# 3rd and 4th attention: the mix with stationary values in four column tiles, both groups of heads in flight, and new turns

## The reference, cut to what matters

```
x -> norm -> 1st attention (8 heads x 32) -> + x -> norm, + a row per batch
  -> state scan over the 1024 rows (64 states, silu), + its output
  -> norm -> 2nd attention (16 heads x 64, causal) -> + x
  -> 3rd attention (16 heads x 16, masked twice) -> + x -> norm
  -> norm -> 4th attention (16 heads x 16, out-of-bounds mask) -> + x
  -> norm -> 256 -> 1024 -> gelu -> 256 -> + x

attention: q = h Wq + bq ; k, v = ctx Wk, ctx Wv
           p = softmax(q k^T / sqrt(hd)) over the 77 keys
           out = concat over heads(p v) Wo + bo
```

## Time and profile before

| | |
|---|---|
| median of 3 runs | 1373.24 us (1370.93 to 1376.13) |
| profiled execution, span from first to last instruction | 1373.0 us |
| PE busy | 1333.4 us, 97% |
| PE weight loads busy (beside PE) | 1124.9 us, 82% |
| DVE busy | 903.9 us, 66% |
| ACT busy | 674.3 us, 49% |
| POOL busy | 558.9 us, 41% |

### The profile page before, as it was taken

One profiled execution on the slowest core, in us unless ns is written; L12 is line 12 of the kernel. 1 busy time (PEld: TensorE's weight loads), 2 busy tenths in 40 slices (PEclk: granted clock), 3 DMA queues, 4 the chain that ended last, 5 costly groups with the idle time before them and its releaser, 6 DMA issues.

```text
span 1373.0 us, 23019 instructions
## 1 busy us (share of the span) xinstructions
PE 1333.4 (97%) x8771; PEld 1124.9 (82%) x8771; DVE 903.9 (66%) x2204; ACT 674.3 (49%) x1495; POOL 558.9 (41%) x700
## 2 busy tenths in 40 slices
PE   7999999999999999999999999999999999899999
PEld 5989987787888788878888888779877987688778
DVE  4778872776756766676576556784768467746771
ACT  4657766134554444544545435445344543464454
POOL 4465431107513643364346211572156216621661
PEclk9999999999999999999999999999999999999999
DMA  4334402200000000000000001000000000000000
GB/s 112 77 112 130 132 21 81 64 8 1 1 16 16 1 13 5 17 0 9 1 9 1 24 5 29 0 1 16 16 1 1 17 16 1 1 5 12 1 1 16
DMA packets 48463, 34.10 MB, mean 25 GB/s; under 512 B 22177, under 2 KB 45536, under 8 KB 48352
## 3 DMA queue, kind: packets, MB, share of 16 engines
q1 hardware_dynamic: 48304, 32.59, 8.5%
q10 hardware_dynamic: 48, 0.01, 0.0%
HBM read 23.26 MB, written 8.39 MB: 23 GB/s over the span
## 4 chain that ended last, share of the span: by engine, by line
PE 84%; DVE 6%; POOL 5%; SPq 2%; ACT 2%; issue 1%; DMA 1%; DVEq 0%; POOLq 0%; ACTq 0%
PE ps L886 11%; PE ps L876 10%; PE ps L836 10%; PE ps L932 8%; PE ps L943 8%; PE ps L855 8%; PE ps L846 6%; PE ps L896 5%; PE ps L802 5%; PE ps L785 4%; PE ps L1037 2%; SPq L611 1%; PE ps L1050 1%; POOL pr L1603 1%; POOL pr L1617 1%
## 5 line engine op out<-in xcount | busy, mean ns | idle before, releaser
L1578 POOL TENSOR_TENSOR rstd<-mv,halfneg 128x1 f32<-128x1 f32 x192 | 109.1, 570 | 340.7 <-DVE mv L1313 338.7
L1617 POOL TENSOR_TENSOR pr<-mx,pr 128x616 f32<-128x616 f32 x128 | 155.9, 1220 | 215.3 <-DVE mx L1347 213.9
L1158 ACT ACTIVATE pr<-pr 128x616 f32<-128x616 f32 x224 | 159.7, 715 | 145.9 <-POOL pr L1617 74.5
L1162 ACT ACTIVATE pr<-ps 128x512 f32<-128x512 f32 x224 | 132.7, 596 | 162.9 <-PE ps L855 162.7
L886 PEld LDWEIGHTS ps<-vtab,pr 128*128 128x128 f32 (+1 forms) x1280 | 153.0, 191 | 14.1 <-ACT pr L1162 10.5
L886 PE MATMUL ps<-vtab,pr 128*128 128x102 f32 (+1 forms) x1280 | 161.9, 275 | 2.0 <-ACT pr L1162 0.9
L855 PE MATMUL ps<-ident,pr 128*128 128x128 f32 (+1 forms) x1120 | 159.4, 275 | 3.5 <-POOL pr L1603 2.7
L1137 ACT ACTIVATE tt<-ps 128x256 f32<-128x256 f32 x160 | 60.9, 383 | 183.5 <-PE ps L785 183.4
L855 PEld LDWEIGHTS ps<-ident,pr 128*128 128x128 f32 (+1 forms) x1120 | 125.5, 139 | 30.1 <-POOL pr L1603 9.1
L876 PE MATMUL ps<-vwo,pr 128*128 128x256 f32 (+1 forms) x640 | 148.9, 381 | 0.0
L1411 DVE TENSOR_TENSOR xt<-xt,ps 128x256 f32<-128x256 f32 x192 | 79.7, 416 | 101.8 <-PE ps L896 50.4
(11 more groups left out here) (200 smaller groups left out, 2368.8 us busy)
## 6 DMA issues: line engine op xcount, KB each, us to landing
out_dram<-xt SPq DMA_DIRECT2D x64, 128.0 KB, 1.7
xt<-in_x_dram SPq DMA_DIRECT2D x32, 128.0 KB, 2.2
xt<-out_dram SPq DMA_DIRECT2D x32, 128.0 KB, 2.1
fc<-in_L_xattn_fc_w_dram SPq DMA_DIRECT2D x2, 1024.0 KB, 6.8
wk<-in_L_xattn_wkv_dram SPq DMA_DIRECT2D x4, 512.0 KB, 5.0
front<-in_L_xattn_wkv_dram SPq DMA_DIRECT2D x4, 512.0 KB, 5.9
wo<-in_L_xattn_wo_dram SPq DMA_DIRECT2D x1, 1024.0 KB, 5.2
kb<-in_L_xattn_wq_dram SPq DMA_DIRECT2D x1, 1024.0 KB, 6.8
```

What stands on the lines that cost most here:

```text
L1158: ac(v, v, ACT.Exp, scale=-ATTN[key[0]].scale).then_inc(done["expo"], 1)
L1162: ac(pr[:, run.lane, 0:4 * P], bank(run.lane, 0), ACT.Copy).then_inc(done["pturn_main"], 1)
L1617: p.tensor_tensor(p8, mx[:, run.lane, :].unsqueeze(2).to_broadcast([P, HG, KEYS]), p8, ALU.subtract).then_inc(done["below"], 1)
```

## The change

The mix of the 3rd and 4th attention swaps its operands. The values are stationary, 32 columns at a time (two heads of 16), and the transposed probabilities stream, 128 columns (the rows of the tile). Four products write the four quarters of the PSUM partitions, so that they lie in four column tiles of the array. A pair of heads spans 154 keys, which lie in two pieces, so each quarter is made by two products (`later` 0 and 1). The result has features on partitions: the turn of the heads and the path through `den_eps` and `heads` after the mix and the copies of the mix's columns go; ACT copies the result to `t` (`mixed`) for `proj`. The normalisation must come ahead of the mix: the 3rd attention gets `rowsum`, `den_eps`, `recip`, `weigh` on DVE, the 4th `rowsum` and `recip` on DVE and a new `scale` on POOL.

All three attentions of 16 heads now have both groups in flight: the second group has its own probabilities (`pr2`, in `front`), its own columns of `mx` and `rec`, its scores wait only for `shift` or `bound` of the first group, and one `mix` and one `resid` serve both. `front` being used for that, the value half of the 2nd attention's kv weights for the second pair is fetched only after the last key product of that pair. All four strings of `TURNS` and that of SP are new, phase 1 and the setup included.

```diff
-COPIES, WCOPY = (3, 2), 160
+SPLIT = 4
+WEIGHED = (L1, L2)
 def attention_steps(a):
...
+    first, second = f"{a.name}.0", f"{a.name}.1"
+    top = ["scores", "rowmax", "shift"] if a is L1 else ["scores", "bound", "rowmax", "below"]
+    masked = ["maskmul"] if a is L2 else []
+    norm = ["rowsum"] + ["den_eps"] * (a is L2) + ["recip", "weigh" if a in WEIGHED else "scale"]
+    turns = ["pturn", "pturn_main", "pturn_rest"]
     steps = [] if a is L1 else [("query", a.name), ("query_bias", a.name)]
...
+    steps += [(s, first) for s in top] + [("expo", first)] + [(s, second) for s in top]
+    steps += [(s, first) for s in masked + norm] + [("expo", second)] + [(s, first) for s in turns]
+    steps += [(s, second) for s in masked + norm + turns] + [("mix", a.name)]
+    return steps + ([] if a is L1 else [("mixed", a.name), ("proj", a.name)]) + [("resid", a.name)]
...
-            vtab[a.name] = sb("vtab" + a.name, [P, PAIR, a.groups, TSLOT[-1], a.hd + 1])
+            vtab[a.name] = sb("vtab" + a.name, [P, PAIR, a.groups, 2 * SPLIT, P // SPLIT])
...
-        vtmp = {"2": front[0:KEYS, 4096:4096 + PAIR * H].rearrange("p (b n) -> p b n", b=PAIR), "3": sb("vtmp3", [KEYS, PAIR, H])[:, :, :]}
+        vtmp = {"2": modrow[0:KEYS, 0:PAIR, :], "3": modrow[0:KEYS, PAIR:2 * PAIR, :]}
...
+        pr2 = front[:, 2048:2048 + LANES * 5 * P].rearrange("p (l n) -> p l n", l=LANES)
...
-                front[:, 0:4096].rearrange("p (k n) -> p k n", k=KC)]
+                front[:, 0:2048].rearrange("p (k n) -> p k n", k=KC)]
...
             def wkv1_get(key, run):
...
-                else:
+                elif part < WKV_PARTS // 2:
                     sp.wait_ge(done["vwo_mm"], at("vwo_mm", f"0{L1.groups - 1}{PAIR - 1}{TILES - 1}"))
...
+                else:
+                    sp.wait_ge(done["k_mm"], at("k_mm", f"11{L1.chunks - 1}"))
...
             def scores(key, run):
...
                 elif a is L1:
-                    pe.wait_ge(done["resid"], at("resid", "1.0", run))
-                else:
-                    pe.wait_ge(done["heads"], at("heads", f"{a.name}.0", run))
+                    pe.wait_ge(done["shift"], at("shift", "1.0", run))
+                else:
+                    pe.wait_ge(done["bound"], at("bound", f"{a.name}.0", run))
...
             def pturn(key, run):
...
+                if group(key):
+                    pe.wait_ge(done["pturn_main"], at("pturn_main", f"{a.name}.0", run))
+                    pe.wait_ge(done["pturn_rest"], at("pturn_rest", f"{a.name}.0", run))
+                elif a is not L0:
+                    s = "shift" if a is L1 else "bound"
+                    pe.wait_ge(done[s], at(s, f"{a.name}.1", run))
...
             def mix(key, run):
...
                     else:
-                        w = a.hd + 1
-                        dst = o[:, TFIRST[j] * w:(TLAST[j] + 1) * w]
-                        src = vtab[a.name][0:TROWS[j], b, g, TSLOT[j]:TSLOT[j + 1], :]
-                        if a is not L0:
-                            heads = TLAST[j] + 1 - TFIRST[j]
-                            n = COPIES[heads - 2]
-                            dst = o[:, 0:n * WCOPY].rearrange("p (k n) -> p k n", k=n)[:, :, TFIRST[j] * w:(TLAST[j] + 1) * w]
-                            src = src.rearrange("p s d -> p (s d)").unsqueeze(1).to_broadcast([TROWS[j], n, heads * w])
-                        last = mm(dst, pt, src, start=j == 0, stop=j == TILES - 1, skip_group_check=True)
+                        w = P // SPLIT
+                        for later in range(2):
+                            for two in range(SPLIT):
+                                j = two + later
+                                last = mm(o[two * w:(two + 1) * w, g * P:(g + 1) * P], vtab[a.name][0:TROWS[j], b, g, later * SPLIT + two, :],
+                                          pt[j], start=not later, stop=bool(later))
...
+            def mixed(key, run):
+                act.wait_ge(done["mix"], at("mix", key, run))
+                ac(t[:, run.lane, :, :].rearrange("p c n -> p (c n)"), bank(run.lane, 0)[:, 0:H], ACT.Copy).then_inc(done["mixed"], 1)
...
             def shift(key, run):
                 dve.wait_ge(done["rowmax"], at("rowmax", key, run))
...
+                if key == "1.1" and run.no == RUNS:
+                    dve.wait_ge(done["vwo_mm"], at("vwo_mm", f"0{L1.groups - 1}{PAIR - 1}{TILES - 1}"))
...
+            def scale(key, run):
+                pool.wait_ge(done["recip"], at("recip", key, run))
+                p8 = heads_view(key, run.lane)
+                p.tensor_tensor(p8, p8, each_head(rec, key, run.lane), ALU.mult).then_inc(done["scale"], 1)
```

More of the change, by code:

```diff
@@ L83, in attention_steps @@
 def attention_steps(a):
-    steps = [] if a is L1 else [("query", a.name), ("query_bias", a.name)]
[L85 to L96, removed]
-        else:
[L98 to L104, removed]
+    if a is L0:
+        steps = [("query", "0"), ("query_bias", "0")]
+        steps += [(s, "0.0") for s in ("scores", "rowmax", "shift", "expo", "pturn", "pturn_main", "pturn_rest", "mix", "recip", "heads")]
+        return steps + [("turn", "0o"), ("turned", "0o"), ("proj", "0"), ("resid", "0")]
+    first, second = f"{a.name}.0", f"{a.name}.1"
[3 more added lines that the diff above has]
+    turns = ["pturn", "pturn_main", "pturn_rest"]
+    steps = [] if a is L1 else [("query", a.name), ("query_bias", a.name)]
+    steps += [(s, first) for s in top] + [("expo", first)] + [(s, second) for s in top]
+    steps += [(s, first) for s in masked + norm] + [("expo", second)] + [(s, first) for s in turns]
+    steps += [(s, second) for s in masked + norm + turns] + [("mix", a.name)]
+    return steps + ([] if a is L1 else [("mixed", a.name), ("proj", a.name)]) + [("resid", a.name)]
 FIRST_NORM = [("load", "x")] + norm_steps("0") + [("prebias", "0")]
@@ L241 @@
[L241 to L245, removed]
@@ L539, in bank, with group, probs, heads_view @@
             return ps[:, 2 * lane + k, :]
+        def group(key):
+            return int(key[2])
+        def probs(key, lane):
+            return (pr2 if group(key) else pr)[:, lane, :]
+        def heads_view(key, lane):
+            return probs(key, lane)[:, 0:HG * KEYS].rearrange("p (h n) -> p h n", n=KEYS)
+        def each_head(small, key, lane):
+            return small[:, lane, group(key), :].unsqueeze(2).to_broadcast([P, HG, KEYS])
         def banks(lane):
@@ L681, in v0_put @@
                 sp.wait_ge(v0_zero, 1)
-                lay_values(sp, L0, vtmp0[:, two, :], vtab["0"][:, two, :, :, :], laid["0"])
+                lay_values(sp, L0, vtmp0[:, two, :], vtab["0"][:, two, :, :, :], laid[f"0{key}"])
             def v_lay(key, run):
@@ L1156, in expo @@
                 act.wait_ge(done[s], at(s, key, run))
-                v = pr[:, run.lane, 0:HG * KEYS]
+                v = probs(key, run.lane)[:, 0:HG * KEYS]
                 ac(v, v, ACT.Exp, scale=-ATTN[key[0]].scale).then_inc(done["expo"], 1)
@@ L1356, in rowsum @@
[L1356 to L1362 removed]
+                s = "maskmul" if key[0] == "2" else "expo"
+                dve.wait_ge(done[s], at(s, key, run))
```

258 lines of the change are left out of this document (134 added, 124 removed).

## The result

The kernel after takes 1398.78 us (median of 4 runs, 1395.1 to 1403.4) against 1372.14 for the one before: a ratio of 1.019, 95% interval 1.016 to 1.022. Forecast were 1316 us, 1285 to 1367. The sign was wrong.

A forecast was written before the change was run, and what follows sets the result against it. PE, busy 97% of 1373.0 us, was taken as the bound: 1373.0 - 78 (mix) + 20 (waits on DVE) + 1 (late weights) = 1316 us. Its own range was 1285 to 1345, widened to 1285 to 1367 to hold 8 in 10.

The forecast's parts named there:

- Bounds, and the mix: PE streams nearly all the time; mix of 3rd and 4th attention falls from 2.42 to 1.205 us, saving 78 us.
- cheap excursions: Mix on PE: leaving the full array could cost as little as 0.20 us, making the saving 86 us.
- leaving the full array: PE around each mix: switching to column tiles and back slows neighbouring steps, taken at 0.325 us per mix.
- rival 2: Mix on PE: half the gain, two tiles at a time or each round's loads exposed; 1360 us, chance 0.13.
- Rivals 1 and 2: Mix on PE: 1, nothing runs side by side, 1464 us, chance 0.13; 2, half the gain, 1360 us, chance 0.13.
- Work moved: Normalisation on other engines: DVE gains 103.4 us, POOL 78 to 89, ACT nothing, all beside PE.
- What cover costs: Second phase: PE waits more often for a DVE at about 80%; taken as 20 us.
- The upper bound of 93: PE waits in second phase: 0.6 points of PE per point of DVE, 15 points more making 93 us.
- the low end: PE waits in second phase: nothing or a small gain, since a lane's chain is shorter.
- Small terms: Late kv weights 1 us; setup and second x loads 0, bounds -3 to +5; second group's first shift 0.
- Late kv weights for the second pair: 2nd attention's value-half weights, fetched after the last key product: 1 us, bounds 0 to 6.
- Rival 3: Second phase: the chain through DVE becomes the bound, waits of 70 to 90 us; about 1370 us, chance 0.10.

The follow-up runs named there:

- e_both: Kernel after with the first phase's order from the kernel before and three x-tile fetches ahead of the 24 value-table transfers; 1360.91 us, 0.9902.
- e_dve: e_both with the scaling of the 4th attention's probabilities on DVE instead of POOL; 1355.78 us, 0.9876.
- e_noweigh: e_both without the multiplications alone: weighing of the 3rd attention (DVE) and scaling of the 4th (POOL) left out; 1328.60 us, 0.9668.
- e_ph1: Kernel after with all engines' order up to the start of phase two taken from the kernel before; 1377.40 us, 1.0026.
- p_new_a: e_dve with the second phase's order searched for anew, table loads counted and 0.05 us to spare at each handing over; 1320.47 us, 0.9608.
- e_mix2: e_both with every mix of the 3rd and 4th attention issued twice; 1407.98 us, 1.0244.

## Why the prediction was wrong

**Bounds, and the mix: right.** PE's queue was the limit, its work fell by 91 us where 78 were forecast (86 with cheap excursions). A mix is 1.02 us, not 1.205, because leaving the full array costs 0.14 and not 0.325. Each of its 32 loads takes 0.11 us, and none shows beside the streams. The estimate from the Trainium skill's 2.38x for three column tiles ("TensorE: Matmul & The Clock Gate", Part 3) was 1.43 us, too much for this case; that page's sentence on which loads overlap, behind rival 2, doesn't hold for column tiles here, where 32 such loads lie within 1.02 us. Rivals 1 and 2 are out.

**Work moved: undersized.** DVE gained 144 us (903.9 to 1047.8), not 103.4; POOL 95, not 78 to 89. The largest part is the weighing, taken at 0.822 us from the earlier trace rows. Groups by form of the kernel after:

```profile
L1410 DVE TENSOR_TENSOR pr<-pr,rec 128x616 f32<-128x616 f32 x64 | 68.9, 1078 | 1.3
...
L1410 DVE TENSOR_TENSOR front<-front,rec 128x616 f32<-128x616 f32 x64 | 66.1, 1034 | 1.4
```

That is 135.0 us where the old count and price make 105.2. The duration goes with POOL: in e_both the 42 weighings with no POOL instruction of over 0.4 us beside them take 0.795 us, the 86 with one 1.183. In the kernel before 47 of 64 had none. Two steps taken as unchanged grew as well: the normed rows of line 1357 from 89 to 107 us (0.41 us each alone, 0.75 beside POOL) and the epsilon from 10 to 21 (sums of single durations, which overlap a little, so that the busy time grew by less). The row sums didn't: 0.783 us with POOL or without. So part of the work given to POOL came back as work on DVE, and e_dve, which takes the scaling off POOL, got part of it back.

**What cover costs: the step that failed.** It took 20 us out of 0 to 93; the runs show 91 in the kernel after, 14 of it the hole on SP, and 74 in e_both. The upper bound of 93 holds by luck: it was drawn by DVE's share of the time, and DVE's share isn't the reason. The argument for the low end, that a lane's chain gets shorter, overlooked that the change puts three or four steps between exponential and transposes, where the 4th had none and the 3rd only `maskmul`; the last one alone is worth 32 us (e_noweigh). And it took for granted that the written-out order would fit the new steps as the old one fitted its own. With an order that fits better, and the 4th's scaling on DVE, the term is 32 us (119.0 less 86.8) and the time 1320, near the 1316. That nearness is in part luck: 12 us more of waiting and 3 of a later start stand against 11 us more of saving on PE (89 in that run, where 78 were forecast). The forecast described what the change can give, not what its order gave.

**Small terms: the other step that failed.** The setup and the loads behind it on SP were put at 0, bounds -3 to +5. The phase began 27 us later, and e_ph1 gives 21 of that back. I had counted the transfers ahead of the second x tiles but not looked for who waits for them: a lane's first statistics, in order on DVE, with PE idle for 10.7 us. The 24 value-table transfers ahead of the gets weren't in the sum at all; the kernel before has as many, but issues its eight gets at 208 to 219 us and the table transfers from 268 us on. Late kv weights for the second pair cost nothing that shows: they are fetched at 817 us, not near 750, and the longest wait of PE from 800 to 850 us is 0.8 us.

**Rival 3** came closest, 1370 us for the paid upper end of the waits; with the two holes the result was 29 us above it. Its name, the chain through DVE, fits: DVE's share of the chain that ended last went from 6% to 33%. Its reason, the load, doesn't. Each failed step alone would have left the sign: with the holes mended the time is 1361 (e_both), and an order like p_new_a's with the holes left in is an estimate of 1320 + 38 = 1358.

## What to carry to other kernels

Where the order of all engines is written out, a change of steps comes with a change of order, and the two must be priced apart: first what leaves the bound engine, then each in-order queue (SP's among them) read for what stands ahead of the first thing that somebody waits for. Here a busy share of 86% beside the bound engine did not stop a gain of 35 us; a step added between two engines' work in each chain cost 32 us, and moving one from the busier engine (0.8 us) to a slower one (1.2 to 1.4 us) cost 27. When judging a new order, run the old kernel with the same treatment as a control.

## What the runs showed of the hardware

- Column tiles in f32: 32 instructions with 32 stationary columns and 128 streamed in 1.02 us, 0.032 each, where one of 128 stationary columns takes 0.110 us; a second such block right behind takes 0.88 (e_mix2). The loads, 0.11 us each, are hidden.
- A DVE operation on two tensors in SBUF, 128x616, takes 0.795 us alone and 1.183 on average beside POOL's work, single ones up to 1.97; a row sum of the same size takes 0.783 in both cases. The Trainium skill ("GPSIMD Engine Reference", Specifications) names DVE instructions with two SBUF inputs among those that contend with POOL, beside those in a 2-port mode; the trace agrees on the first, and which mode an instruction ran in no trace here shows.
- A table load on ACT is 1.283 us for each turn between exponential and gelu, and stands in the engine's order.
- The granted clock fell from the 2.4 GHz level towards 1.2 where PE stood idle: a mean of 0.76 from 40 to 60 us and of 0.66 from 300 to 320, stretches in which PE was busy for 8.2 and 5.8 of 20 us. It stayed low for a while after PE went on: the first score step behind the hole of 14 us took 2.47 us from start to start, one at the 2.4 GHz level takes 1.17. Before, it never left the top digit.
